# Four recurrent layers over eight items, one search beside the next item: semaphores that count on, a loop written out, and another order of steps

## The reference, cut to what matters

```
for each layer:                      # L0, L1, L2, L3
    xn = layernorm(x)
    s  = attn(xn)                    # L0 delta-rule recurrence, L1 time mix with decay,
                                     # L2 selective state space, L3 top-k softmax attention
    g  = silu(ffn(xn))               # L0, L3 coupling net, L1 local attention of depth 2,
                                     # L2 two of four experts
    x  = x + s * g
```

```
aw = softmax(q @ k.T / sqrt(D)); kth = top_k(aw, 25)[..., -1:]
aws = aw * (aw >= kth);          aws = aws / (aws.sum(-1) + 1e-8)
o = a * (aws @ v) + (1 - a) * linear_attention(q, k, v)
```

## Time and profile before

| | |
|---|---|
| median of 3 runs | 5127.44 us (5120.69 to 5140.48) |
| the profiled execution, its own time | 5138.43 us |
| its span in the profile | 5136.6 us |
| TensorE busy | 3962.0 us, 77% |
| VectorE busy | 3993.4 us, 78% |
| ScalarE busy | 2973.6 us, 58% |
| GpSimd busy | 2537.6 us, 49% |
| granted TensorE clock, mean | 0.837 |

### The profile page before, as it was taken

One profiled execution on the slowest core, in us unless ns is written; L12 is line 12 of the kernel. 1 busy time (PEld: TensorE's weight loads), 2 busy tenths in 40 slices (PEclk: granted clock), 3 DMA queues, 4 the chain that ended last, 5 costly groups with the idle time before them and its releaser, 6 DMA issues. The chain is left out here.

```text
span 5136.6 us, 59306 instructions
## 1 busy us (share of the span) xinstructions
PE 3962.0 (77%) x17112; PEld 1870.6 (36%) x17112; DVE 3993.4 (78%) x7866; ACT 2973.6 (58%) x5751; POOL 2537.6 (49%) x2332
## 2 busy tenths in 40 slices
PE   7776878878877777867788687886888778787676
PEld 2332344323443244422444234432344324342233
DVE  4326797877978788786888779887887868978698
ACT  4444666656665566655666566665666556665543
POOL 1204465445645355463654536544555535646365
PEclk9887889888888898978889798988888888997655
DMA  2000000000000000000000000000000000000000
GB/s 82 1 25 3 3 1 25 1 3 3 1 26 0 3 3 1 25 1 5 1 1 25 3 3 1 25 1 3 3 1 25 1 3 3 1 25 1 3 1 3
DMA packets 8147, 44.15 MB, mean 9 GB/s; under 512 B 864, under 2 KB 864, under 8 KB 7392
## 3 DMA queue, kind: packets, MB, share of 16 engines
q1 hardware_dynamic: 7776, 39.89, 2.0%
HBM read 37.52 MB, written 2.36 MB: 8 GB/s over the span
## 5 line engine op out<-in xcount | busy, mean ns | idle before, releaser
L2031 DVE MAX8 m<-top 128x8 f32<-128x512 f32 x2048 | 1295.2, 680 | 6.1 <-ACT top L1965 5.9
L2094 POOL TENSOR_SCALAR top<-top,m 128x512 f32<-128x512 f32 x512 | 819.3, 1600 | 791.8 <-DVE m L2031 682.1
L2035 DVE MATCH_REPLACE8 top<-m,top 128x512 f32<-128x512 f32 x1536 | 1027.1, 677 | 0.4
L2100 POOL TENSOR_TENSOR top<-top 128x512 f32<-128x512 f32 x512 | 655.2, 1280 | 20.1 <-ACT top L1973 1.7
L290 PE MATMUL bank<-arena,weights 128*128 128x512 f32 (+5 forms) x992 | 526.1, 649 | 100.1 <-DVE arena L1217 44.8
L290 PE MATMUL bank<-arena,consts 128*128 128x512 f32 (+1 forms) x864 | 546.2, 722 | 56.1 <-POOL arena L1638 30.5
L1904 PE MATMUL bank<-consts,top 128*128 128x128 f32 x2048 | 394.8, 325 | 230.1 <-POOL top L2100 173.9
L290 PE MATMUL bank<-arena 128*64 128x128 f32 (+3 forms) x3200 | 469.6, 370 | 55.8 <-ACT arena L1080 51.3
L1904 PEld LDWEIGHTS bank<-consts,top 128*128 128x128 f32 x2048 | 279.7, 165 | 499.0 <-POOL top L2100 351.2
L1980 ACT ACTIVATE top<-bank 128x512 f32<-128x512 f32 x512 | 305.5, 597 | 263.0 <-PE bank L1904 262.7
L1965 ACT ACTIVATE top<-bank 128x512 f32<-128x512 f32 x512 | 302.9, 593 | 251.2 <-PE bank L290 172.8
(11 more groups left out here) (300 smaller groups left out, 6484.2 us busy)
## 6 DMA issues: line engine op xcount, KB each, us to landing
arena<-experts_dram SPq DMA_DIRECT2D x32, 768.0 KB, 6.6
weights<-weights_dram SPq DMA_DIRECT2D x1, 6013.0 KB, 22.5
hold<-x_dram SPq DMA_DIRECT2D x9, 256.0 KB, 2.7
out_dram<-x_out SPq DMA_DIRECT2D x9, 256.0 KB, 3.4
consts<-consts_dram SPq DMA_DIRECT2D x1, 1759.5 KB, 8.7
rot<-consts_dram SPq DMA_DIRECT2D x1, 1024.0 KB, 24.3
weights<-weights_dram SPq DMA_DIRECT2D x1, 969.0 KB, 4.8
```

The costliest lines, as they stand in the source:

```text
L2031: nc.vector.max(m8[:, slot(p, e), k], src).then_inc(SB["top"], 1)
L2035: nc.vector.match_replace(wk_[e], m8[:, slot(p, e), k], sc[slot(p, e)] if k == 0 else wk_[e], -3e38).then_inc(SB["rest"], 1)
L2094: nc.gpsimd.tensor_scalar(pp[e], sc[slot(p, e)], m8[:, slot(p, e), TOPK // 8, 0:1], None, ALU.is_ge).then_inc(SB["kept"], 1)
L2100: nc.gpsimd.tensor_tensor(pp[e], pp[e], ex[e], ALU.mult).then_inc(SB["pp"], 1)
```

## The change

Three things change. The waits take a `floor` for each semaphore, the sum of all that was raised on it in the blocks before; a semaphore so counts on over the items, and `clear` is called once, at the end of the program. A wait for a transfer goes through `landed`, which multiplies by 16. Since the counts to wait for now differ from item to item, the hardware loop is a Python loop: seven blocks stand one behind the other in the program. And the table `SEARCH` has other digits in 106 of its 192 places.

```diff
     def layer(self, **names):
-        own = Layer()
+        own = Layer(self.floor)
...
-                own.sem[name], own.base[name], own.total[name] = self.sems[key], self.ends.get(key, 0), int(total)
+                own.sem[name], own.key[name], own.base[name], own.total[name] = self.sems[key], key, self.ends.get(key, 0), int(total)
...
     def settle(self):
...
+            for n, t in own.raised.items():
+                self.floor[own.key[n]] = self.floor.get(own.key[n], 0) + t
             own.raised = {}
...
-        return self.sem[name], self.base[name] + count
+        return self.sem[name], self.floor.get(self.key[name], 0) + self.base[name] + count
+
+    def landed(self, name, count=1):
+
+        sem, value = self(name, count)
+        return sem, 16 * value
...
-SEARCH = ("0210020250210111101110113034221131412302512101102011202012023110m50112251100421133202211010010021201"
+SEARCH = ("02010202502101111002110202603220322322213131000210211311012031l3143011141012221133210003111101012200"
...
-                    pe.wait_ge(SD.sem["x0"], 16)
+                    pe.wait_ge(*SD.landed("x0"))
...
             late_marks.settle()
-            clear([*marks.sems.values(), *top_marks.sems.values(), *(late_marks.sems.values() if first else ())])
...
         lead_marks.settle()
-        clear(top_marks.sems.values())
         run(0, True, False)
-        with nc.Fori(1, B) as b:
+        for b in range(1, B):
             run(b, True, True)
         run(B, False, True)
...
                     sp.wait_ge(S.sem["out"], 16)
+        clear([*marks.sems.values(), *top_marks.sems.values(), *late_marks.sems.values()])
```

More of the change, by code:

```diff
@@ L181, in __init__ @@
         self.nc, self.ctx, self.label = nc, ctx, label
-        self.sems, self.ends, self.layers = {}, {}, []
+        self.sems, self.ends, self.layers, self.floor = {}, {}, [], {}
     def layer(self, **names):
-        own = Layer()
+        own = Layer(self.floor)
         for engine, text in names.items():
@@ L200, in settle, with __init__ @@
             assert not wrong, wrong
+            for n, t in own.raised.items():
+                self.floor[own.key[n]] = self.floor.get(own.key[n], 0) + t
             own.raised = {}
 class Layer:
-    def __init__(self):
-        self.sem, self.base, self.total, self.raised = {}, {}, {}, {}
+    def __init__(self, floor):
+        self.floor, self.sem, self.key, self.base, self.total, self.raised = floor, {}, {}, {}, {}, {}
     def __getitem__(self, name):
@@ L216, in __call__ @@
         assert 0 < count <= self.total[name], (name, count)
-        return self.sem[name], self.base[name] + count
-SEARCH = ("0210020250210111101110113034221131412302512101102011202012023110m50112251100421133202211010010021201"
-          "01101111020022021221100031212000313100610421106221332305002020100021101210110000100011001132")
+        return self.sem[name], self.floor.get(self.key[name], 0) + self.base[name] + count
[3 more added lines that the diff above has]
+SEARCH = ("02010202502101111002110202603220322322213131000210211311012031l3143011141012221133210003111101012200"
+          "01020102011121021221100041013000313121312131223221214330103100112010012000010120101010011132")
 def weave(a, b):
@@ L378, in pe @@
                 S, n = self.S, self.n
-                for sem, count in self.ready:
-                    pe.wait_ge(sem, count)
+                for layer, name, count in self.ready:
+                    pe.wait_ge(*layer(name, count))
                 mm(self.xc, C("centre"), self.src).then_inc(S[n + "_xc"], 1)
@@ L697, in build @@
         lead_marks = Marks(nc, ctx, "b")
-        lead_marks.sems = top_marks.sems
+        lead_marks.sems, lead_marks.floor = top_marks.sems, top_marks.floor
         lead = Opening(lead_marks.layer(**OPENING))
@@ L710, in __init__ @@
                 L.cp = Coupling(S0, "L0", 0, xn0, A[3], [L.carve() for _ in range(6)], L.carve(8))
-                L.norm = Norm(S0, "on", L.osb, [S0("osb", 1)], L.og, L.sq, L.rs, W("l0_ln_g"), sg, idle=A[2])
+                L.norm = Norm(S0, "on", L.osb, [(S0, "osb", 1)], L.og, L.sq, L.rs, W("l0_ln_g"), sg, idle=A[2])
         Layer0 = Layer0()
@@ L846, in __init__ @@
                 L.fin = [xn[:], L.f, L.f]
-                L.lx = Norm(S1, "xn", x[:], [S0("x_new", 1)], xn[:], L.sq, L.rs)
-                L.lf = [Norm(S1, f"ffn{i}", L.hs, [S1("hs2_a", i + 1), S1("hs2_b", i + 1)], L.nrm, L.sq, L.rs)
+                L.lx = Norm(S1, "xn", x[:], [(S0, "x_new", 1)], xn[:], L.sq, L.rs)
+                L.lf = [Norm(S1, f"ffn{i}", L.hs, [(S1, "hs2_a", i + 1), (S1, "hs2_b", i + 1)], L.nrm, L.sq, L.rs)
                       for i in range(DEPTH)]
@@ L1328, in __init__ @@
                 L.xg = [spare[4], L.xr]
-                L.lx = Norm(S2, "xn", x[:], [S1("x_new", 1)], xn[:], L.sq, L.rs)
+                L.lx = Norm(S2, "xn", x[:], [(S1, "x_new", 1)], xn[:], L.sq, L.rs)
         Layer2 = Layer2()
@@ L1366, in l2_pe @@
                     if k == 0:
-                        pe.wait_ge(SD.sem["weights"], 16 * NE)
+                        pe.wait_ge(*SD.landed("weights", NE))
                     if n:
@@ L2075, in search_dve @@
             v.wait_ge(*SB("m", 1))
-            v.wait_ge(SD.sem["stored"], 16)
+            v.wait_ge(*SD.landed("stored"))
             tt(x_out[:], x_b[:], og, ALU.add).then_inc(SB["x_out"], 1)
@@ L2266, in _ @@
                         sp.dma_start(x0, x_in[b + 1]).then_inc(SD["x0"], 16)
-                        sp.wait_ge(SD.sem["x0"], 16)
+                        sp.wait_ge(*SD.landed("x0"))
                         sp.wait_ge(*S1("attn", DEPTH))
```

## The result

The changed kernel takes 5083.69 us (median of 18 runs, 5057.39 to 5129.93), the one before 5135.64 in as many. The ratio is 0.9918, with a 95% interval of 0.9897 to 0.994: faster by 42 us (interval 31 to 53), where 101 were forecast. The medians alone lie 52 us apart. The time lies in the range, but by the ratio less than half of the forecast gain came.

A forecast was written before the change was run, and what follows sets the result against it. VectorE was nearest to the bound: 498 us of work plus 113 us standing still per item. Seams 55, warmer restart 6 and order 40 sum to 101 us off the profiled 5138.4, or 5026 us from the median; range 4945 to 5098.

The forecast's parts named there:

- The seam: Between items: without clears, second barrier and jump, 7.7 us gained at six seams, 3.9 at two without a jump.
- the rival in which it stays: Branch still heads each block, only clears and barriers go: 5057 us with the order's gain, 5097 without; chance 0.06.
- Fetching the written-out program: Instruction fetch of the written-out blocks: costed at nothing, since the loop's body is already fetched anew every pass.
- The clears at the end: At the program's end the clears stay, behind the store instead of ahead of it: nothing gained or lost.
- What the seams bring as a whole: All seams, item 0's opening and the end: 55 us, plus 6 us for a warmer TensorE restart.
- the clock's term: TensorE's first matmul pairs after a seam run warmer because it idles less: 6 us in all.
- L1583 to L1590: Stretch behind the expert loop: three search steps in the first gap, none in the second; gain 1 us an item.
- TensorE's restart: After each seam, shorter idle may leave TensorE's first matmul pairs warmer: 6 us taken, between nothing and 18 us.
- Part 2: New order of search steps among the layers' steps: 5.7 us an item, 40 us in seven.
- Expert loop: VectorE's waits at the expert product, 10.0 us an item, fall to 2.3 by even spacing: gain 7.7 us.
- Attentions: Empty gaps behind row maxima: one appears in the first attention, one goes ahead of the second; net 0.
- only the seams pay: Rival: new gaps cost elsewhere what they give in the expert loop; 5072 us, chance 0.17.

The follow-up runs named there:

- seams_old_order: The changed kernel with the old SEARCH table, so new seams only; 5087.66 us, ratio 0.9901 to the kernel before.
- new_from_experts: The changed kernel with SEARCH entries 0 to 133 from the old table, the rest new; 5068.46 us, ratio 0.9866.

## Why the prediction was wrong

**Right.**
- *The seam, 7.7 us each and 3.9 without a jump.* 8.31 us became 0.39, 7.9; TensorE's idle at the other two went from 5.88 to 1.86 us and from 5.79 to 1.85, 4.0. The jump's stall is 4.3 us of it, as counted, so that the rival in which it stays is out.
- *Fetching the written-out program, nothing.* Less is fetched, and nothing waits for it.
- *The clears at the end, nothing.* From its first matmul the last block takes 362.8 us (4695.98 to 5058.8), against 362.9 before (4773.74 to 5136.6).
- *What the seams bring as a whole.* Forecast 61 us with the clock's term, measured 51, interval 40 to 62. That is the sum of 65 us gained in place and some lost behind it (in the profiles 17 in the first attentions alone), so the agreement is in part luck.
- *L1583 to L1590, 1 us.* From L1588 to L1598 VectorE was idle for 4.6 us with the old table and is for 4.0.

**Mis-sized.** *TensorE's restart, 6 us between ends of 0 and 18.* It was the upper end at the seam itself: the first pairs lost 0.98 and 0.89 us. After 5.51 us idle they were still cold, after 1.85 warm. The stage of L0 with its seam is 9.2 us shorter with the old table (102.9 to 93.7), where 8.5 were forecast.

**Wrong, first: Part 2, "Expert loop ... Gain 7.7 us".** It came to 3.4. I priced VectorE's waits one gap after another and read TensorE's fullness only as an argument for a rival: 27.9 of 30 us. The same row, taken as a floor, has the answer: 27.94 / 30 of the 58.6 us from the first to the last product is 54.6, so at most 4.0 us could go. The waits did what the new spacing promised on TensorE's side (81.6 to 34.9 us) and came back on ScalarE's, whose silu needs TensorE's product (19.4 to 42.5). That is 4.3 us an item, 30 of the 59 that are missing. (Two slips of the working change nothing in this: two gaps of 0.6 and one of 1.2 us are 2.4, not 2.3, and with the 19.2 us of the earlier trace rows for the attentions, not 20.6, 66 us were left alone and not 64.)

**Wrong, second: "Attentions ... 0", and with it the sum itself.** By the table above the second projections and the second attention cost 3.2 us an item instead of 3 (that sum came out by luck, since restoring the digits of entries 77 to 113 with the gaps named gives 0.3 back), while 1.7 us came off the first attention and 1.7 off VectorE's own work, neither of which I had in the sum. The profiled execution so ends at 5060.55, 78 us under the one before: 47 of them are the seams' (the profiled execution of seams_old_order took 5091.6), where 61 were forecast, and 31 the order's, where 40 were. The other 23 us are between it and its median, and no row of one trace holds them. An item's length goes with TensorE's clock in its attentions, and this changes when the item starts a little later. The working priced every gap at one value and the clock once a seam; it is priced anew in each item, and by more (91.0 to 97.7 us in one stage) than what most digits move. In the kernel before this was to be seen: its first attentions took 90.9 to 91.2 us five times and 94.6 and 94.8, in items of the same code, and its seven stretches differed by 11 us. How much of the missing gain the clock took is not shown beyond this.

The order's worth is so no fixed number. By medians (some from different chips), new table against old, it is -1 us in the old loop, -4 in the changed program, -46 with warmed attentions, -13 with four idle matmuls; for the mixed table of new_from_experts it is -19, and -73 with the four matmuls. By the ratios these are -4, +9, -47, -19, -18 and -69, each to within some 15 us. The forecast's 40 is within that spread, and the changed kernel is at its poor end. Of the rivals, "only the seams pay" has the time nearest to the measured one, 5072, and its reason is half of the true one: the gaps weren't paid for elsewhere one by one, TensorE was full, and for the rest its clock is what the runs point to.

**What stays open.** Some of the 18 times of the changed kernel would fit a number of long items that differs between executions, at 19 us each (two in the profiled one, 5060; two or three more make 5099 to 5118), others, such as the five from 5070 to 5078, would not; only one execution was traced. And no run tells ahead of time which table or which shift gives a good start.

## What to carry to other kernels

Before pricing the waits of one engine, take the busy time of the engine waited for in the same stretch as a floor: a stretch in which that engine is busy for 94% can get shorter by 6% and no more. Where a granted clock takes values between 0.5 and 1 in a stage, compare the lengths of that stage over the repeats of the loop first: their spread says what a small reordering may win or lose by its start alone, and an edit worth less than that needs many executions, not one trace. Branches back and bundles of semaphore clears at a seam are the surest money: 7.9 us each here with a jump and 4.0 without one, all of it found in its place, and 51 us of it in the whole time.

## What was not expected of the hardware

- The same 474 matmuls in the same list took some 91, 92.7, 94.8 or 97.7 us and no length in between, at 0.76 to 0.87 in the shortest and 0.69 in the longest. The Trainium skill, TensorE: Matmul & The Clock Gate (What's actually happening), says that the gate judges activity in windows that run free of the program, so that the point of change depends on where in one the work lands. The shifts fit that without proving it: 6 us of added work in all made one program 38 us faster by the medians, another 15 us slower.
- The same page of the Trainium skill calls the cost of warming up under 1% of a typical span. Here the spread between executions of one program, which went with their clock, was 1.4% (5057 to 5130 us), and the one between two shifts of one program 0.7%.
- TensorE after 1.85 us of rest at a seam made its first pair in 1.10 us; after 5.51, 5.88 and 9.77 us in 2.04, 2.05 and 2.08.
- VectorE's L1593 took 2.20 us at the median before (1.23 to 2.20), its counterpart L1601, with a search step between it and L1598, 1.22 us in all eight. What stood beside it differs. Before, GpSimd ran L2100 and L2094 all through it, and its own L2094 took 2.54 us there where the one 3 us earlier took 1.57; in the changed kernel GpSimd did nothing in that time:

```profile
2235.93 2.20 DVE L1593 TENSOR_TENSOR arena<-arena 128x1024 f32<-128x1024 f32 x1
...
2234.13 1.57 POOL L2094 TENSOR_SCALAR top<-top,m 128x512 f32<-128x512 f32 x1 [8.97 <-DVE m L2031]
2235.78 1.27 POOL L2100 TENSOR_TENSOR top<-top 128x512 f32<-128x512 f32 x1
2237.02 2.54 POOL L2094 TENSOR_SCALAR top<-top,m 128x512 f32<-128x512 f32 x1
...
2217.61 1.22 DVE L1601 TENSOR_TENSOR arena<-arena 128x1024 f32<-128x1024 f32 x1
```

  It is so in all seven items of the kernels with the old digits there and of those with the new ones, and item 0, which has no search beside it, took 1.23 us before too. L1590 (1.36 us beside GpSimd) became L1598 (1.23 us without) in the same way. So the order gained 1.1 us of VectorE's own work an item by moving two instructions away from GpSimd's; no run varied that by itself.
